# Reordering the list building, moving a spread of node numbers, and loading registers for six windows at once in a four-layer graph kernel

## What is computed

```
for layer in (sage, gat, runge_kutta, rel):      # x += layer(relu(layernorm(x)))
sage:  three times  h = h @ W_self + (segment_sum(h[src], dst) / deg) @ W_neigh + b   (relu between)
gat:   xt = h @ W;  alpha = leaky_relu(a_src[src] + a_dst[dst]), softmax over each target
       out = segment_sum(xt[src] * alpha, dst)          (4 heads of 32)
runge_kutta: y = h + (k1 + 3(k2 + k3) + k4) / 8,  k = f(..),
       f(y) = segment_sum(y[src3] * e3, dst3) over the edges taken both ways, e normed by target
rel:   out = relu(segment_sum(norm * (h[src] @ W_rel[type]), dst) + h @ W_loop + b)
```

## Time and profile before

| | us |
|---|---|
| median of 3 runs | 13578.29 (13573.32 to 13611.32) |
| the profiled execution | 13585.59 |
| its span | 13583.8 |
| PE busy | 10090.9 |
| DVE busy | 7971.0 |
| POOL busy | 6409.9 |
| ACT busy | 3712.1 |

### The profile page before, as it was taken

How to read it: one execution, slowest core, us unless ns; L and a number is a source line. 1 busy time by engine, 2 the same in 40 slices (tenths; PEclk the granted TensorE clock), 3 DMA queues, 4 the chain that set the end, 5 groups by cost and what they waited for, 6 DMA issues and landing times.

```text
span 13583.8 us, 192267 instructions
## 1 busy us (share of the span) xinstructions
PE 10090.9 (74%) x68184; PEld 8162.2 (60%) x68289; DVE 7971.0 (59%) x13503; ACT 3712.1 (27%) x6670; POOL 6409.9 (47%) x6626
## 2 busy tenths in 40 slices
PE   6796067758665788764689868986998699899444
PEld 3675067657654333454688768876887688644333
DVE  8754066436444888777688646764676477600334
ACT  0242040220313577532332033203320332154000
POOL 0277776777773677300045603460455045501776
PEclk8665599989988999998999999999999999999555
DMA  1000087556663333322799768876887688776222
GB/s 54 2 4 18 16 269 227 177 182 190 207 194 107 110 106 107 88 81 81 248 310 314 203 214 281 294 203 215 287 287 204 215 294 272 244 297 254 53 53 56
DMA packets 1073032, 2382.23 MB, mean 175 GB/s; under 512 B 199212, under 2 KB 385888, under 8 KB 1045028
## 3 DMA queue, kind: packets, MB, share of 16 engines
q0 software_dynamic: 354208, 926.60, 25.0%
q10 hardware_dynamic: 403392, 811.55, 17.0%
q1 hardware_dynamic: 314564, 632.22, 13.1%
HBM read 1211.29 MB, written 1158.47 MB: 174 GB/s over the span
## 4 chain that ended last, share of the span: by engine, by line
PE 39%; POOL 26%; issue 15%; DVE 11%; DMA 7%; ACT 1%; DVEq 1%; ACTq 0%; POOLq 0%; SPq 0%
PE ps L2024 15%; PE ps L2044 14%; POOL list L739 6%; POOL list_f L739 6%; POOL rows_work L760 6%; POOL rows_work L771 5%; PE ps L2134 5%; POOL rows_work L795 3%; DMA rows_work<-messages_R,rows_R 2%; DVE rows_work L1507 2%; DMA rows_work<-near 2%; DMA rows_work<-messages_F,rows_R 2%; PE ps L1957 1%; PE ps L2036 1%; DMA ADM<-near 1%
## 5 line engine op out<-in xcount | busy, mean ns | idle before, releaser
L2024 PE MATMUL ps<-H,onehot 128*128 x23760 | 3191.4, 286 | 1038.2 <-DVE rows_work L1507 535.3
L795 POOL DMA_INDIRECT rows_work<-messages_F,rows_R x1890 | 1828.1, 967 | 4038.5 <-DMA messages_F<-rows_work 2640.3
L2024 PEld LDWEIGHTS ps<-H,onehot 128*128 128x128 f32 x23760 | 2905.3, 196 | 1243.9 <-issue 1174.4
L2044 PE MATMUL ps<-rows_work,onehot 128*128 128x128 f32 (+1 forms) x15840 | 2157.0, 282 | 329.6 <-DMA rows_work<-messages_F,rows_R 193.1
L932 ACT CAST onehot<-rows_work 128x512 f32<-128x512 uint8 x1980 | 1222.5, 618 | 3818.9 <-PE ps L2024 2515.0
L2044 PEld LDWEIGHTS ps<-rows_work,onehot 128*128 128x128 f32 x15840 | 1951.6, 192 | 496.8 <-issue 446.8
L1507 DVE TENSOR_TENSOR rows_work<-ps,list_words 128x512 f32<-128x512 f32 x2160 | 1484.4, 688 | 847.3 <-PE ps L2024 847.0
L1515 DVE TENSOR_TENSOR onehot<-ps,list_words 128x512 f32<-128x512 f32 x1980 | 1355.7, 688 | 599.4 <-PE ps L2044 581.3
L760 POOL DMA_INDIRECT rows_work<-rel_table,rows_F x832 | 788.0, 947 | 967.6 <-DMA rel_table<-list_words 714.4
L739 POOL DMA_INDIRECT list<-list_words,rows_R x831 | 812.9, 978 | 849.3 <-DVE rows_R L1273 576.2
L795 POOL DMA_INDIRECT rows_work<-messages_R,rows_R x1080 | 1021.1, 946 | 388.0 <-issue 261.7
(11 more groups left out here) (350 smaller groups left out, 10981.2 us busy)
## 6 DMA issues: line engine op xcount, KB each, us to landing
messages_F<-rows_work ACTq DMA_DIRECT2D x630, 792.0 KB
messages_R<-rows_work ACTq DMA_DIRECT2D x360, 792.0 KB
rel_table<-list_words SPq DMA_DIRECT2D x196, 1024.0 KB, 3.8
rows_work<-onet SPq DMA_DIRECT2D x480, 192.0 KB
gat_rows<-rows_work SPq DMA_DIRECT2D x220, 264.0 KB, 2.1
rows_work<-gat_rows SPq DMA_DIRECT2D x220, 264.0 KB, 2.7
ADM<-onet SPq DMA_DIRECT2D x240, 192.0 KB
rows_work<-near SPq DMA_DIRECT2D x180, 192.0 KB
```

The costliest lines, as they stand in the source:

```text
L795: pool.indirect_dma_start(out=ring2[:, G2 % RING2, :], out_offset=None, in_=rows_dram[PASSES[r]], in_offset=bass.IndirectOffsetOnAxis(ap=t ...
L2024: ins = mm(ps[:, G1 % 3, j * P:(j + 1) * P], onet_f[G1 % 2][:, j * P:(j + 1) * P], hflat[:, bass.ds(at["blocks"][g % GPW], FEAT)], start=T ...
L2044: ins = mm(into, member, ring2[:, G2 % RING2, j * AUX:j * AUX + width], start=False, stop=True, skip_group_check=True)
```

## The change

Three things are edited. (1) On DVE and PE the cell list's work comes first: both block numbers, the cell count, `records`, the prefix sums and chunks, and only then F's count, totals and ranks. POOL's scatter of list R waits for the first count of `records_ready`; two waits for F's records stand ahead of `run_gathers`. `count_src` gets another place. PE waits for the last cell chunk before F's products. (2) ACT's spread of the node numbers moves from ahead of the other spread to behind `copy_turned(3)`; DVE's copy of them moves behind the attention products and the PEAK flag; SP's copy of list F moves behind the PEAK table and waits for `rows_named`. (3) `window_words` loads the words of six windows (18 groups) at once, `slots_of` in attention those of four windows, and `firsts_of` there four instead of two.

The core of the diff; the moved blocks of DVE and PE are the same lines at another place:

```diff
+NAMED = 6
+LOOKED = 4
...
-        count_src = place(3330, CU * CB // 2).bitcast(BF16).rearrange("p (s n) -> p s n", s=CU)
+        count_src = place(EW * 10, CU * CB // 2).bitcast(BF16).rearrange("p (s n) -> p s n", s=CU)
...
-        def slots_of(engine, key, w):
+        def slots_of(engine, key, w, n=1):
-                slot_of[key][:, w * TABLE + 1:w * TABLE + WINDOW], engines=(engine,),
+                slot_of[key][:, w * TABLE:(w + n) * TABLE].rearrange("o (w j) -> o w j", j=TABLE)[:, :, 1:WINDOW], engines=(engine,),
...
         def window_words(engine, n, w, words):
-                windows_of[n][:, w * WTAB + words.start:w * WTAB + words.stop], engines=(engine,),
+                windows_of[n].rearrange("o (w j) -> o w j", j=WTAB)[:, w:w + min(NAMED, WIN - w), words], engines=(engine,),
...
                 if name == "gat":
                     sp.dma_start(block_of, block_dram.rearrange("(o t) -> o t", o=1)).then_inc(blocks_loaded, 16)
+                if name == "peak":
+                    sp.wait_ge(rows_named, 2)
                     sp.dma_start(list_keep, list_words[:, 0:TILES * W]).then_inc(list_kept, 16)
-                if name == "peak":
                     for q in range(QUADS):
...
                 if c % (BATCH * CC) == 0:
-                    pool.wait_ge(records_ready, CI + c // (BATCH * CC) + 1)
+                    pool.wait_ge(records_ready, c // (BATCH * CC) + 1)
...
             scatter_list_2()
+            pool.wait_ge(records_ready, CELL_CHUNKS // BATCH + CI)
+            pool.wait_ge(spare_ready, 2)
...
             act.wait_ge(nodes_copied, 1)
-            spread(nodes_out, nodes_in, node_base, nodes_spread)
             spread(fetch_out, fetch_in, None, rows_spread)
...
             root_of(1)
             copy_turned(3)
+            spread(nodes_out, nodes_in, node_base, nodes_spread)
             act.wait_ge(peak_consts, 1)
...
             st(norm_relu(1))
-            dve.wait_ge(nodes_spread, BLOCKS)
-            st(v.tensor_copy(lists["F"][:, :, 2], nodes_out[:, 0:TILES]))
             dense(3)
...
             dve.wait_ge(table_ready, parts_through("peak"))
+            dve.wait_ge(nodes_spread, BLOCKS)
+            v.tensor_copy(lists["F"][:, :, 2], nodes_out[:, 0:TILES]).then_inc(rows_named, 1)
+            dve.wait_ge(rows_named, 2)
...
+            pe.wait_ge(cell_totalled, CELL_CHUNKS)
+            pe.wait_ge(cell_read, 2 * CELL_CHUNKS)
+            mm(ps[:, 6, 0:CB], ones[0:EP, :], zeros[0:EP, 0:CB], start=True, stop=False)
...
+                if w % LOOKED == 0:
+                    offsets["looked"] = slots_of(mybir.EngineType.PE, name[-1], w, min(LOOKED, WINDOWS - w))
+                offsets["next"] = offsets["looked"][w % LOOKED * (WINDOW - 1):(w % LOOKED + 1) * (WINDOW - 1)], None
...
-                    elif w % 2 == 0:
-                        offsets["firsts"] = firsts_of(mybir.EngineType.PE, key, w, 2)
+                    elif w % LOOKED == 0:
+                        offsets["firsts"] = firsts_of(mybir.EngineType.PE, key, w, min(LOOKED, WINDOWS - w))
...
+                if g % (NAMED * GPW) == 0:
+                    at["blocks"] = window_words(mybir.EngineType.PE, "FR".index(PASSES[m]), w, slice(0, GPW))
                 if g % GPW == 0:
-                    at["blocks"] = window_words(mybir.EngineType.PE, "FR".index(PASSES[m]), w, slice(0, GPW))
...
+                if g % (NAMED * GPW) == 0:
+                    at["slots"] = window_words(mybir.EngineType.PE, n, w, slice(3, 5))
                 if g % GPW == 0:
-                    at["slots"] = window_words(mybir.EngineType.PE, n, w, slice(3, 5))
```

More of the change, by code:

```diff
@@ L1287, in _ @@
                     name_rows_1(t)
[L1289 removed]
+            dve.wait_ge(records_ready, CELL_CHUNKS // BATCH)
             spare = to_row["R"][:, LIVE:EC]
             v.tensor_tensor(spare, spare, spare_1, ALU.add).then_inc(spare_ready, 1)
+            m0 = 0
+            with dve.Fori(0, CI) as i:
+                for t in range(CU):
+                    members("F", i, t, m0)
+            dve.wait_ge(counts_closed, 1)
+            st(v.tensor_reduce(small[:, 0, :], ps[:, 6, 0:CB].rearrange("p (c b) -> p b c", b=BLOCKS), AX, ALU.add))
@@ new lines, in _ @@
+            m0 += CHUNKS
+            with dve.Fori(0, CI) as i:
+                st.enter(i, 3 * CU + 3)
+                for t in range(CU):
+                    members("F", i, t, m0)
+                for t in range(CU):
+                    dve.wait_ge(chunk_summed, i * CU + (m0 + t + 1 + CU))
+                    rank3 = rank_t.rearrange("p (c b) -> p c b", b=BLOCKS)
+                    ahead = ps[0:EP, t % 3, 0:CB]
+                    ahead3 = ahead.rearrange("p (c b) -> p c b", b=BLOCKS)
+                    st(v.tensor_tensor(ahead3, ahead3, carry[0:EP, :].unsqueeze(1).to_broadcast([EP, CT, BLOCKS]), ALU.add))
+                    st(v.tensor_tensor(rank_t, ahead, member_bf[:, t, :], ALU.mult))
+                    st(v.tensor_reduce(pos_f[:, t * CT:(t + 1) * CT], rank3, AX, ALU.add), False)
+                    v.tensor_tensor(carry, carry, ps[:, 3 + t % 3, 0:BLOCKS], ALU.add).then_inc(chunk_ranked, 1)
+                    dve.wait_ge(chunk_ranked, i * CU + (t + 1 + 2))
+                st(v.tensor_copy(key_n, pos_f))
+                st(v.tensor_scalar(key_q, key_n, 7, None, ALU.arith_shift_right))
+                st(v.tensor_scalar(key_n, key_n, P - 1, None, ALU.bitwise_and))
+                v.scalar_tensor_tensor(out=to_row["F"][:, bass.ds(i * CU * CT, CU * CT)], in0=key_n, scalar=float(TILES),
+                                       in1=key_q, op0=ALU.mult, op1=ALU.add).then_inc(records_ready, 1)
+                st.leave(CI)
@@ L1909, in _ @@
                     same_chunk(t + 1)
+            pe.wait_ge(cell_totalled, CELL_CHUNKS)
+            pe.wait_ge(cell_read, 2 * CELL_CHUNKS)
+            mm(ps[:, 6, 0:CB], ones[0:EP, :], zeros[0:EP, 0:CB], start=True, stop=False)
+            with pe.Fori(0, CI) as i:
+                for t in range(CU):
+                    pe.wait_ge(chunk_members, i * CU + (t + 1))
+                    mm(ps[:, 6, 0:CB], ones[0:EP, :], member_bf[:, t, :], start=False, stop=False, skip_group_check=True).then_inc(chunk_summed, 1)
+            mm(ps[:, 6, 0:CB], ones[0:EP, :], zeros[0:EP, 0:CB], start=False, stop=True).then_inc(counts_closed, 1)
+            with pe.Fori(0, CI) as i:
+                for t in range(CU):
+                    pe.wait_ge(chunk_members, i * CU + (CHUNKS + t + 1))
+                    pe.wait_ge(chunk_ranked, i * CU + (t + 1))
+                    rank, total = ps[:, t % 3, 0:CB], ps[:, 3 + t % 3, 0:BLOCKS]
+                    mm(rank, earlier[0:EP, :], member_bf[:, t, :], start=True, stop=False)
+                    for c in range(CT - 1):
+                        rest = CT - 1 - c
+                        mm(rank[:, (c + 1) * BLOCKS:].rearrange("p (c b) -> p c b", b=BLOCKS), ones[0:EP, :],
+                           member_bf[:, t, c * BLOCKS:(c + 1) * BLOCKS].unsqueeze(1).to_broadcast([EP, rest, BLOCKS]),
+                           start=False, stop=True, skip_group_check=True)
+                    mm(rank, ones[0:EP, :], zeros[0:EP, 0:CB], start=False, stop=True)
+                    for c in range(CT):
+                        ins = mm(total, ones[0:EP, :], member_bf[:, t, c * BLOCKS:(c + 1) * BLOCKS], start=(c == 0), stop=(c == CT - 1))
+                    ins.then_inc(chunk_summed, 1)
             pe.wait_ge(gat_mixed, 4)
```

137 lines of the change are left out of this document (45 added, 92 removed).

## The result

The changed kernel takes 13458.34 us (median of 4 runs, 13427.59 to 13467.86), the kernel before 13577.67 (4 runs): a ratio of 0.9896 (95% interval 0.988 to 0.9913). The direction held, the size did not.

A forecast was written before the change was run, and what follows sets the result against it. No engine was taken to bound the whole (PE 39%, POOL 26% of the wait chain). Terms -322 - 45 - 255 - 36 + 132 + 25 = -501 from 13585.6 gave 13084.6, said as 13,080 us; range 12,880 to 13,340.

The forecast's parts named there:

- Part one: Cell list first: first scatter moves from 578.9 to 252 us, chunks keep their length; -322 us, between -327 and -246.
- lower clock in the late F stage: Rival: PE at its lower clock in F's rank steps makes the list wait for DVE; +76 us, 13,155; chance 0.08.
- Part two: Node numbers later: root and peaks come 58 us earlier, POOL held once after 16 gathers; -45 us.
- Weighted sums: Attention: four loads of 1.70 us, each partly hidden, become one of 6.3; +25 us, between -30 and +80.
- five passes -255: Messages alone (passes 1, 2, 5, 7, 9): windows of 3.3 us plus merged load; -51 us a pass.
- Passes 0 and 3: Passes that also build one-hots, in a loop estimated at 3.9 us a window; -18 us each, -36 together.
- Beside sums: Passes 4, 6, 8, 10: six windows take 38.6 us for 36.1; +37 in three, +22 in pass 4, +132 together.
- Stores bind: Rival: windows of passes alone stay at 3.9 us and the merged stall eats the rest; -210 us, 13,370; chance 0.13.
- Queues hide more: Rival: windows of 3.1 us alone, nothing lost beside sums; -765 us, 12,813; chance 0.15.
- Every word pays 0.79: Slower rival: on PE's sequencer every word behind DMA issues costs 0.79 us, 18 words 14.2; 14,815; chance 0.03.
- Per instruction: Rival: a register load costs per instruction, not per word, 18 words 0.8 + 1.6 us; 12,490; chance 0.05.
- bound of -325: Fast bound for the five passes of messages alone, at windows of 3.1 us; the other bound was 0.

The follow-up runs named there:

- e3: Edits (1) and (2) on the kernel before, six windows' words merged only for messages of passes 1, 2, 5, 7 and 9: 13070.49 us, ratio 0.9618.
- e6: e5 with POOL scattering the first 40 columns of list F ahead of its first gathers of the sums: 12571.36 us, ratio 0.9252.
- e1: Edits (1) and (2) alone on the kernel before, every register load left as it was there: 13227.9 us, ratio 0.9727.
- e4: e1 with PE loading the next window's three message words two groups later, at the third group of a window: 12851.67 us, ratio 0.9451.
- e7: e1 with three windows' words a load in every pass (9 words for messages, 6 for sums): 13417.1 us, one run.
- e10: e6 with eight adjacent words a load, for messages and for an attention window's first block and seven slots: 12407.96 us, ratio 0.9138.
- e8: e1 with two windows a load, all eight words of each, 16 adjacent words: 13186.06 us, one run.
- e5: e4 with, beside sums, message words loaded at a window's second group and the sums' words at their third: 12613.37 us, ratio 0.9274.

## Why the prediction was wrong

- *Part one (-322 forecast, -310 measured).* Right up to the chunks. The 327 us up to the prefix sums came as 326; the fifteen chunks up to the first scatter, which were to keep their length, took 15.6 us more (125.3 for 109.7). PE's granted clock in them was 0.93, then 0.60, where it had been 0.73 and 0.76. I did not test that, but the traces of the experiments that have the new order run the same code up to there, and they differ: in e3 and e6 the clock was 0.97 throughout and the first scatter came at 241.9; in e1, e4 and e7, with 0.68 to 0.80 in the last 58 us, it came at 268 to 274. So the 12 us lie within what one and the same code does. The rival of a lower clock in the late F stage cost nothing: the clock did fall there (0.57 from 1100 to 1200, 0.50 behind), but DVE was ready for the list 105 us early. Its last row numbers came at 789 and not at 873, with a clock of 0.79 from 268 to 600, where 579 to 1000 had had 0.66.
- *Part two (-45 forecast, -42 measured from the end of the sums of pass 2 to the last gather of the peaks; -44 from there to pass 3 in e1).* Right, the one hold by SP's queue included.
- *Weighted sums (+25 forecast, +48 measured).* Price right, cover wrong: e10 shows that this stage follows PE's sequencer, so a load of 6.84 is hardly hidden, where the four of 1.70 had been hidden in part (48 us in 27.5 merged loads is 1.7 each).
- *Passes 1 and 2 (2 x -51 forecast, 0 measured).* The step that failed is "five passes -255". The passes did get that much shorter; POOL's list F scatter, which I described as lying "between the passes", was already the later one. I never looked at who releases the sums of pass 1.
- *Passes 5, 7, 9 (-51 each; -50, -50, -48).* The size is right and its make-up not: windows are 2.94 and not 3.3, a merged load costs 7.1 and not 4.8. Two errors that cancelled, so the hit is luck. I had the DMA engines as the bound at 3.0 to 3.3 and no price for the clock.
- *Passes 0 and 3 (-18 each forecast; +42, +41).* The step "a loop that I estimate at 3.9 us a window" failed: with cheap loads the loop takes 4.3 (387 / 90, e4). The load of 2.4 was almost wholly covered there (4.6 a window), so merging took the cover away and gave almost nothing back: 30.4 us for six windows, where one load a window makes 27.8.
- *Beside sums (+22 and 3 x +37 forecast; +62, +55, +54, +52).* The term "6 x 5.65 + 4.7 = 38.6" is 6 x 5.53 + 6.9 = 40.1. The stalls were mis-sized: by the sum under e7 the queue covered 1.8 and not 2.1 of each load, and I had left out the half-speed stretch behind them.
- *The rivals.* None of them was it. "Stores bind" gives 13,370, near the measured time, but by a mechanism that isn't there: the windows alone fell to 2.94. "Queues hide more" falls with the 6.9. "Every word pays 0.79" falls: the added 1.6 us are fixed per load, as forecast (e7: nine words 2.2 clear of the issue, 3.84 behind it). "Per instruction" falls for words with a stride and is nearer for adjacent ones (16 in 1.10).
- *A sum.* The bound of -325 is added up wrongly: at windows of 3.1 the terms give 6 x 3.1 + 4.75 = 23.35 for 28.0, or -350. "Queues hide more" is some 25 us too high by it.

The kernel before had already shown the cheap form of a load. I took the price of a word from 0.53, 0.77, 1.70 and 1.84 us and left the last layer aside, where PE loads eight adjacent words at a time:

```profile
L539 PEldq TENSOR_LOAD <-tables x110: 592/596/607, 12511.2 to 13560.7; - x110
```

And ACT's 0.78 is not of ten words: the fifth load of `spread` has the nine that are left of 49. The loads of ten took 0.99 us (the very first 1.19) from word 0 or 20, and 2.2 from word 10 or 30.

The gap of 377 us is thus passes 1 and 2 (105), passes 0 and 3 (119), beside sums (91), attention (24), the list (12) and passes 5, 7 and 9 (5); the other 21 lie in the gaps between the stages.

Not settled: what about SP's issue holds a load up (the issue, or the transfer that it starts); what the half-speed stretch costs beside sums; and why e8's loads of 2.74 in the passes alone are not covered at all.

## What to carry to other kernels

A short stall that the queue covers is free however often it comes; merged into a long one it is covered once, and where the tensor engine then stood still for 5 us the clock dropped as well. Before merging, ask what makes each small one dear: here its place just behind another engine's DMA issue, and words taken with a stride; moving it by a group and loading adjacent words gained what merging lost. And before booking a shorter stage, look at who releases the next one.

## What the runs showed of the hardware

- A register load costs some 0.24 us a word with a stride (6 words 1.50, 12 2.92, 28 6.84), and two or three adjacent words are no cheaper (0.53, 0.77). Longer runs of adjacent words are, if they begin at the right place: 8 words 0.59 and 16 words 1.10 from a multiple of eight, ten words 0.99 from word 0 or 20. They are not from word 10 or 30 (ten words 2.2) or from one past a multiple of eight (seven words 1.70). The starts that were cheap are all multiples of four. The Trainium skill, "Runtime: NRT & Kernel Launch", section Instruction fetch mechanics, has about 200 ns a register even in bulk; the strided loads are near it, the 16 adjacent words at 0.07 each are not, and the measurement decides.
- A load that runs close behind SP's issue of a DMA is longer by an amount that does not grow with its words. Begun 0.1 us behind it, 3 words take 2.37 for 0.77, 9 words 3.84 for 2.22 and 16 words 2.74 for 1.10; begun 1.5 to 2.0 behind it, two words take 1.56 for 0.53 (e4); from 2.0 to 2.5 us behind it three words take 0.87, and from 2.5 on 0.77. Some 0.3 us behind ACT's issue it was not longer (0.54 us for two words in e5).
- After the standstills of PE behind a merged load (5.1 us in pass 5) the granted clock was 0.50 for some 3 us alone and 6 us beside sums. The kernel before, with 1.47 us in every window, had kept 0.97.
